# Another order of the steps of a gated-attention and spiking-FFN kernel on all five engine queues

## The reference, cut to what matters

```python
x = x + tanh(g_xattn) * mlstm(layernorm(x), ctx, ctx)       # q = layernorm(x), k = v = ctx
x = x + tanh(g_ffn)   * ffn(layernorm(x))

def mlstm(q, k, v):                                         # for each batch
    ig, fg = [q, k, v] @ igate_w.T + b, [q, k, v] @ fgate_w.T + b      # (8, 256)
    cs = cumsum(log_sigmoid(fg))
    log_D = where(tril, cs[:, s] - cs[:, t], -inf) + ig[:, t]          # (8, 256, 256)
    D = exp(log_D - max_t(log_D))
    C = (q_h @ k_h.T) / sqrt(32) * D
    h = C / (max(abs(C.sum(-1)), exp(-max_t(log_D))) + 1e-6) @ v_h
    return layernorm(h) * ln_scale

def ffn(x):                                                 # W_fc (1024, 256), W_proj (256, 1024)
    y = square(relu(x @ W_fc.T)) @ W_proj.T
    # 5 steps of mem = 0.9*mem + y - reset, spike = mem > 1
    return number_of_spikes(y) / 5
```

## Time and profile before

| What | Value |
|---|---|
| median of 3 runs | 660.52 us (660.26 to 661.48) |
| profiled execution, first to last instruction | 661.2 us |
| PE busy | 589.5 us, 89%, 6032 matmuls |
| DVE busy | 542.4 us, 82% |
| POOL busy | 485.6 us, 73% |
| ACT busy | 484.4 us, 73% |
| mean granted clock of TensorE | 0.972 |
| DMA | 71.33 MB, mean 108 GB/s |

### The profile page before, as it was taken

One profiled execution on the slowest core, in us unless ns is written; L12 is line 12 of the kernel. 1 busy time (PEld: TensorE's weight loads), 2 busy tenths in 40 slices (PEclk: granted clock), 3 DMA queues, 4 the chain that ended last, 5 costly groups with the idle time before them and its releaser, 6 DMA issues.

```text
span 661.2 us, 17665 instructions
## 1 busy us (share of the span) xinstructions
PE 589.5 (89%) x6032; PEld 483.9 (73%) x6032; DVE 542.4 (82%) x1222; ACT 484.4 (73%) x1011; POOL 485.6 (73%) x531
## 2 busy tenths in 40 slices
PE   1265887799999999999999999999999999999795
PEld 0155776778787878787788878787878777787684
DVE  4878787889989998899989998999888998958522
ACT  4555777678787888788878878788878867676463
POOL 6157678867996969787897799787969788675232
PEclk9996799999999999999999999999999999999898
DMA  8915553845276335916573538642680556300000
GB/s 262 225 52 115 97 115 70 176 83 96 83 156 169 74 91 147 208 26 139 115 186 60 96 110 155 159 86 80 150 207 18 97 101 148 63 2 33 1 33 32
DMA packets 73192, 71.33 MB, mean 108 GB/s; under 512 B 8720, under 2 KB 68752, under 8 KB 73104
## 3 DMA queue, kind: packets, MB, share of 16 engines
q1 hardware_dynamic: 71888, 70.00, 47.3%
q10 hardware_dynamic: 1216, 0.21, 0.2%
HBM read 27.44 MB, written 8.39 MB: 54 GB/s over the span
## 4 chain that ended last, share of the span: by engine, by line
PE 51%; DVE 10%; issue 10%; ACT 7%; POOL 7%; SPq 4%; DMA 2%; POOLq 0%; ACTq 0%; DVEq 0%
PE z_ps L997 16%; PE y_ps L1057 16%; PE arg_ps L702 3%; PE qk_ps L717 3%; POOL sq_lo L1040 3%; DVE spikes L1075 3%; PE misc_ps L463 2%; SPq L650 2%; PE misc_ps L529 2%; SPq L513 2%; ACT sq_hi L1019 1%; POOL c_lo L746 1%; PE pv_ps L766 1%; PE pv_ps L764 1%; PE pv_ps L841 1%
## 5 line engine op out<-in xcount | busy, mean ns | idle before, releaser
L1040 POOL TENSOR_TENSOR sq_lo<-w_raw,sq_hi 128x512 fp32r<-128x512 f32 (+1 forms) x96 | 113.0, 1178 | 66.2 <-ACT w_raw L1020 66.1
L746 POOL TENSOR_TENSOR c_lo<-decay 128x512 bf16<-128x512 f32 x128 | 132.5, 1042 | 22.4 <-DVE decay L736 22.2
L997 PE MATMUL z_ps<-x_hi,wfc_hi 128*128 128x512 f32 (+1 forms) x288 | 115.7, 402 | 5.9 <-ACT w_raw L1007 4.1
L1057 PE MATMUL y_ps<-sq_hi,wpr_hi 128*128 128x512 f32 (+1 forms) x288 | 115.1, 400 | 1.1 <-POOL sq_lo L1040 1.1
L997 PE MATMUL z_ps<-x_hi,wfc_lo 128*128 128x512 f32 (+1 forms) x288 | 107.2, 372 | 0.0
L997 PE MATMUL z_ps<-x_lo,wfc_hi 128*128 128x512 f32 (+1 forms) x288 | 107.2, 372 | 0.0
L1057 PE MATMUL y_ps<-sq_lo,wpr_hi 128*128 128x512 f32 (+1 forms) x288 | 106.8, 371 | 0.0
L1057 PE MATMUL y_ps<-sq_hi,wpr_lo 128*128 128x512 f32 (+1 forms) x288 | 106.6, 370 | 0.0
L736 DVE TENSOR_TENSOR decay<-qk_ps,decay 128x512 f32<-128x512 f32 x128 | 87.1, 680 | 18.5 <-PE qk_ps L717 14.4
L728 ACT ACTIVATE decay<-arg_ps,lqk_col 128x512 f32<-128x512 f32 x128 | 86.5, 676 | 19.7 <-PE arg_ps L705 19.1
L1040 POOL TENSOR_TENSOR sq_lo<-relu,sq_hi 128x512 fp32r<-128x512 f32 (+1 forms) x48 | 56.3, 1173 | 37.9 <-ACT relu L1020 35.2
(11 more groups left out here) (139 smaller groups left out, 1686.2 us busy)
## 6 DMA issues: line engine op xcount, KB each, us to landing
x_in<-x SPq DMA_DIRECT2D x32, 256.0 KB, 3.5
kT_in<-ctx_cols SPq DMA_DIRECT2D x32, 256.0 KB, 3.8
v_in<-ctx_rows SPq DMA_DIRECT2D x32, 256.0 KB, 3.2
k_stack<-kT_hi SPq DMA_DIRECT2D x64, 128.0 KB, 3.4
k_stack<-kT_lo SPq DMA_DIRECT2D x64, 128.0 KB, 3.7
q_stack<-qT_hi SPq DMA_DIRECT2D x64, 128.0 KB, 4.0
q_stack<-qT_lo SPq DMA_DIRECT2D x64, 128.0 KB, 4.2
out<-w_raw SPq DMA_DIRECT2D x32, 256.0 KB, 3.6
```

The costliest lines, as they stand in the source:

```text
L746: e.tensor_tensor(c_lo[i % NCH][:, :], c, top(c), ALU.subtract).then_inc(sem("c_lo"), 1)
L997: ins = e.matmul(z_ps[:, tokens(q)], lhsT, rhs, start=(n == 0), stop=(n == len(terms) - 1))
L1040: e.tensor_tensor(sq_lo[n % NSQ][:, tokens(q)], relu[n % NRE][:, tokens(q)], sq_hi[n % NSQ][:, tokens(q)].bitcast(fp32), ALU.subtract).the ...
L1057: ins = e.matmul(y[:, c, :], w[:, j, c * P:(c + 1) * P], h, start=(j == 0 and i == 0 and (c == 0 or whole)), stop=(j == FT - 1 and i == 2) ...
```

## The change

Every engine's list of steps is written in another order. Each engine executes the same steps with the same instructions, tiles and waits as before: 211 steps on SP, 704 on ACT, 583 on DVE, 806 on PE and 514 on POOL. In the new order 166 steps stand in other places among SP's (by 11 places at most), 322 of ACT's (6), 228 of DVE's (15), 370 of PE's (9) and 369 of POOL's (15). The steps of the start are reordered, the loop bodies are reordered (the loops run to 5, on SP to 6), and what comes after is written out; from z_step(15, 4) on, about the last 60 us, the order is what it was on all engines. `misc_order` is adapted to the new turns. Line numbers after are two higher.

```diff
         def sync_program(e):
             load_x(e, 0)
-            load_k(e, 0)
             load_x(e, 1)
+            load_k(e, 0)
...
             for n in SLOTS:
-                load_k(e, 4 * n + 6)
                 stack_heads(e, 4 * n + 2)
                 store(e, 2 * n - 2)
                 load_x(e, 4 * n + 6)
+                load_m_rows(e, 4 * n + 2)
...
```

More of the change, by code:

```diff
@@ L1442, in vector_program @@
             am_split(e, 1, 3)
+            q_lo(e, 4)
             cmul(e, 0, 2)
             state_own(e, 0)
-            ln1_stats(e, 6)
-            q_lo(e, 4)
             split_wpr_lo(e, 0)
@@ L1509, in vector_program @@
             cmul(e, 4, 3)
-            q_lo(e, 8)
             out_step(e, 0)
-            for n in SLOTS:
+            for n in range(1, 6):
                 state_own(e, 4 * n)
@@ new lines, in vector_program @@
+            x2_lo_step(e, 23)
+            ln1_stats(e, 31)
+            spikes_step(e, 11, 0)
+            ln1_offset(e, 15)
+            cmul(e, 26, 0)
+            spikes_step(e, 11, 1)
+            spikes_step(e, 11, 2)
+            spikes_step(e, 11, 3)
+            x2_lo_step(e, 24)
+            spikes_step(e, 11, 4)
+            cmul(e, 26, 1)
+            out_step(e, 11)
+            h_norm(e, 25)
+            ln2_stats(e, 25)
+            q_lo(e, 30)
+            cmul(e, 26, 2)
+            x1_step(e, 25)
@@ new lines, in tensor_program @@
+            gate_products(e, 29)
+            y_step(e, 11, 5)
+            state(e, 25)
+            arg(e, 26, 0)
+            x2_T(e, 23)
+            qk(e, 25, 3)
+            y_step(e, 11, 6)
+            y_step(e, 11, 7)
+            qk(e, 26, 0)
+            x2_T(e, 24)
+            arg(e, 26, 1)
+            z_step(e, 12, 0)
+            inter(e, 25)
+            arg(e, 26, 2)
+            qk(e, 26, 1)
+            z_step(e, 12, 1)
+            pv(e, 25, 0)
+            pv(e, 25, 1)
+            z_step(e, 12, 2)
@@ new lines, in tensor_program @@
+            q_T(e, 30)
+            count_T(e, 11)
+            arg(e, 26, 3)
+            qk(e, 26, 2)
+            z_step(e, 12, 3)
+            y_step(e, 12, 0)
+            z_step(e, 12, 4)
+            y_step(e, 12, 1)
+            gate_products(e, 30)
+            z_step(e, 12, 5)
+            state(e, 26)
+            q_T(e, 31)
+            qk(e, 26, 3)
+            y_step(e, 12, 2)
+            inter(e, 26)
+            arg(e, 27, 0)
+            pv(e, 26, 0)
+            pv(e, 26, 1)
@@ new lines, in tensor_program @@
+            y_step(e, 13, 5)
+            state(e, 29)
+            arg(e, 30, 0)
+            x2_T(e, 27)
+            qk(e, 29, 3)
+            y_step(e, 13, 6)
+            y_step(e, 13, 7)
+            qk(e, 30, 0)
+            x2_T(e, 28)
+            arg(e, 30, 1)
+            z_step(e, 14, 0)
+            inter(e, 29)
+            arg(e, 30, 2)
+            qk(e, 30, 1)
+            z_step(e, 14, 1)
+            pv(e, 29, 0)
+            pv(e, 29, 1)
+            z_step(e, 14, 2)
+            count_T(e, 13)
```

1038 lines of the change are left out of this document (780 added, 258 removed), and 3 rows, old and new, of the table order.

## The result

The changed kernel took 671.86 us in the median of 4 runs (668.29 to 672.86), against 660.57 for the kernel before, measured beside it; the ratio is 1.0157, with a 95% interval of 1.0131 to 1.0183. 653.7 us was forecast. Ratios and intervals in this document are taken over all executions of the two kernels that were measured side by side, so they are not quite the quotient of the medians, and single executions far off (743.87 us of stats_back, 3056.9 of b_pool, 933.98 of the kernel before) are left out.

The account below looks back on a forecast made before the run. PE was taken to bound the slots, chains through several engines the start. -5.2 us for the slots and -1.6 for the start on the profiled 661.2 gave 654.4, a median of 653.7; range given 647.5 to 661.8.

Parts of the forecast that it names:

- the claim on z_step(2n+1, 0): In each slot, PE's wait for x2_lo on DVE shrinks by 0.1 us, bounds 0 and 0.27.
- DVE's chain to x1_step(15): In the slots, q_lo(20) ahead of x1_step(15), which releases state(16), holds the gain at about 0.6 us.
- Rival (a): DVE sets the slots: q_lo ahead of x1_step takes back 0.6 us a slot; median 657.6, chance 0.16.
- Rival (c): Row loads m_rows come late behind other transfers on SP's queue, 1.5 us a slot; median 662.7, chance 0.17.
- the single stalls: PE's stalls before state(9) and state(21), 1.16 and 0.65 us, were to go.
- the four waits that were priced: PE's waits before count_T(5), qk(14, 2), arg(15, 1), z_step(7, 0): together 0.91 us a slot, 0.6 forecast as gain.
- The slots' gain: The repeated slots: -3.9 for small waits, +0.5 for changes of kind, -1.8 for v_lo, together -5.2 us.
- count_T's 0.3: In each slot, count_T ahead of arg(4n+2, 3) gains 0.3 us of two waits, bounds 0 and 0.40.
- arg(4n+3, 1)'s 0.2: In each slot, arg(4n+3, 1) behind inter gains 0.2 us of its wait for ACT, bounds 0 and 0.24.
- v_lo's 1.8 us: Earlier v_lo_step(4n+1) on POOL removes the stalls before state(9) and state(21): 1.8 us, bounds 0.7 and 1.8.
- The start: Before the slots: -0.5 for load_x(1), -1.6 for q_lo(4), +0.5 for POOL, together -1.6 us, bounds +2.1 and -2.9.
- The tail: The last 60 us keep their order and were worth nothing.

Follow-up runs that it names:

- stats_back: The changed kernel with ln1_stats(4n+8) on VectorE back behind cmul(4n+2, 3), as in the kernel before: 656.72 us, ratio 0.9921.
- b_pool: The kernel before with GpSimd's whole order of the changed kernel and nothing else: 671.93 us, ratio 1.0141.
- a_act: The changed kernel with ln3_apply(4n+2) ahead of ln1_rstd(2n+4) again on ScalarE: 669.25 us, ratio 1.0093.
- a_pool: The changed kernel with k_hi(4n+8) and v_hi_step(4n+4) on GpSimd moved behind square_lo(2n+1, 0): 667.26 us, ratio 1.0061.
- a_dve: The changed kernel with ln3_stats(4n+2) on VectorE right behind x1_step(4n+2), ahead of ln1_stats(4n+8) and cmul(4n+3, 1): 660.88 us, ratio 0.9980.
- stats_back_2: stats_back measured once more, for a profile at the full clock: 657.67 us, ratio 0.9953.
- a_all: The changed kernel with the edits of a_act, a_pool and a_dve together: 663.37 us, ratio 1.0005.
- best_order: stats_back with ln1_stats(4n+8) on VectorE two steps later, behind q_lo(4n+7): 661.75 us, ratio 0.9993.
- before_vlo_count: The kernel before with v_lo_step(4n+5) right behind v_hi_step(4n+5) on GpSimd and count_T(2n-1) ahead of arg(4n+2, 3) on TensorE: 660.11 us, ratio 0.9995.
- before_two: The kernel before with ln1_stats(4n+8) and cmul(4n+3, 1) ahead of ln3_stats(4n+2) on VectorE, ln1_rstd(2n+4) ahead of ln3_apply(4n+2) on ScalarE: 667.62 us.
- before_again: The kernel before, unchanged, run once more for a second profile: 662.77 us for the profiled execution, median of its eight executions 662.27.
- after_clo: The changed kernel with am_split(n+3, 3) and c_lo_step(4n+3, 1) exchanged on GpSimd: 672.42 us, ratio 1.0143.
- stats_back_ln3: stats_back with ln3_stats(4n+2) also moved ahead of cmul(4n+3, 1) on VectorE: 657.7 us, ratio 0.9930.

## Why the prediction was wrong

- **The step that failed** is the claim on z_step(2n+1, 0), "DVE's steps before it move by little", and with it the premise that "an order can give back only the moments in which PE waits": nothing was put down for what it can take. The prediction followed only places where PE waited before, and DVE's chain to x1_step(15). x2_T(4n+2) had 1.2 us to spare and was not followed; ln1_stats(4n+8) and cmul on DVE, ln1_rstd on ACT and GpSimd's run took them and 2.5 more. a_act, a_pool and a_dve shorten that wait each by the link that they undo, and the step back takes it away whole (stats_back_2). In time the links on VectorE count: ln1_stats left a place where DVE had been idle for one where it was packed (1.0 us a slot), and ln3_offset was held for 2.45 us instead of 0.33 in stats_back_2 (2.1 us a slot).
- **Rival (a)**, DVE sets the slots, had the right engine and the wrong place (q_lo(20)) and sign. Rival (c) had the right sign and the wrong queue: the row loads cost 1.0 us in all, and the slots aren't better with SyncE's old order.
- **The waits were not all found.** The list of PE's waits of before, from 134 to 600, has two entries that the prediction leaves out in whole or in part:

```profile
PE pv_ps L808 <- issue: 1.9, 3, 1.0
PE pv_ps L841 <- POOL s_lo L829: 0.9, 5, 0.2
```

  The first is the single stalls, and there are three, not two: state stops for a further 0.40 us at 487.50. The second is inter waiting for state_lo, about 0.3 us in every slot with the overlap, as long as the longest of the four waits that were priced. In the changed kernel it is gone: qk stands ahead of inter there.
- **The slots' gain** of 5.2 us was not seen in that form. stats_back_2, where the stall is out, needs 423.2 us for the six, 3.2 less than before. Of this 1.8 us lie in the sixth slot alone, behind the loop (69.85 to 68.07 us), and a_act, a_pool, a_dve, a_all and best_order have that 68.1 as well. In the loop its slots take 70.8 us in the median, against 71.25 before, and before_vlo_count, with two moves only, has 70.8 too. stats_back_2 has waits of its own, 1.9 us for q_lo at the gate products and 1.8 for m_rows. In the changed kernel the gain is 426.4 + 13.4 - 437.0 = 2.8 us, with about 3 us lost to the clock. count_T's 0.3 and arg(4n+3, 1)'s 0.2 us are gone as forecast; z_step(2n+1, 0)'s wait, 0.27 to 0.30 before, was 0.11 to 0.31 us in the changed kernel and under 0.05 in the loop of stats_back_2.
- **v_lo's 1.8 us** went from the trace and not from the times: a term read from one profiled execution. If that one, like the others, took 1.8 us more than its span of 661.2, it was 2.5 us above the median, not the 0.7 that I took from its span.
- **The start**: gate_products(3) was there at 44.87, 1.9 us earlier than 46.81, as reckoned. But gate_products(4) then waited 1.68 us, pv(1, 0) was 1.6 us late, and z_step(2, 0) came out 0.7 earlier for the 1.6 forecast. The other kernels with this start had it between 133.8 and 136.7, and those with the old one between 133.8 and 135.7 (before_two, before_again, before_vlo_count): a gain in the start isn't shown.
- **The tail**: nothing, as forecast.

## What to carry to other kernels

Where queues are ordered by hand, the price of a move isn't read from the waits that are there, but from the slack of every consumer behind it: list for each step of the bounding engine how long its producers were done, and follow those with less than what is put ahead of them. Look at what an instruction waits for before it is put ahead of another that doesn't need it, and at idle stretches on a moved step's engine: the step belongs there. A wait that gets shorter is not yet time won: a_act took 1.4 us off PE's wait in each slot and PE waited for the same VectorE at count_T, 5 us later, so compare the length of the slot, and where the engine that releases stands. And the span of a profile is not a time; terms of 1 or 2 us that stand at single places should be seen in a second execution.

## What the runs showed of the hardware

ln3_offset, a VectorE instruction of 128x2 numbers with both inputs in SBUF, took 0.13 to 0.28 us where it did not wait, 1.02 behind one GpSimd instruction and 2.45 behind a run. In each of the 17 traces the 17 to 25 instructions of its line (L374, L376) that took over 0.3 us ended within 0.06 us of the end of a GpSimd instruction. cmul, one of whose inputs is in PSUM, took 0.66 to 0.69 us beside GpSimd at work. The Trainium skill, "SBUF — State Buffer", section "Who interferes with whom", holds that VectorE and GpSimd share a pair of ports under an exclusive lock, and that a VectorE instruction with two SBUF inputs contends with a GpSimd instruction that reads SBUF, while one with at most one does not, outside VectorE's two-port modes. The traces agree, with 2.45 against 0.15 us. They add that VectorE wasn't always let in between two GpSimd instructions: not ahead of k_weigh, kT_hi and v_hi in the changed kernel and in after_clo, nor ahead of k_weigh in a_pool, but ahead of k_weigh in best_order, where ln3_offset took 1.08 us. What decides it stays open.

TensorE's granted clock fell to 0.50 for 3.4 us behind three of the five stalls of 2.5 us in the changed kernel. Behind the stalls of 0.8 us (a_dve), 1.1 (a_act) and 1.4 (a_pool) it stayed 1.00, but in stats_back_ln3 it fell behind one single wait of 1.4 us, before gate_products at 439.36.
